# Graph layer with segment maximum: every neighbour row fetched by GpSimd, none rebuilt by TensorE

## What is computed

```
theta_x = (x[dst] - x[src]) @ theta_w.T + theta_b
phi_x   = x[src] @ phi_w.T + phi_b
e       = relu(theta_x + phi_x)
out     = segment_max(e, dst)          # nodes without an edge: 0
result  = layernorm(x + out)
```

## Time and profile before

| | before |
|---|---|
| median of 3 runs | 1052.79 us |
| the profiled execution's own time | 1051.62 us |
| its span, first to last instruction | 1049.1 us |
| mean granted TensorE clock | 0.848 of full speed |
| busy: GpSimd (POOL) | 780.5 us, 74% of the span |
| busy: TensorE (PE) | 705.6 us, 67% |
| busy: VectorE (DVE) | 642.4 us, 61% |
| busy: ScalarE (ACT) | 326.6 us, 31% |
| moved by DMA | 250.69 MB, mean 239 GB/s |

### The profile page before, as it was taken

The page is one execution under the profiler, slowest core; times in us unless marked ns, Lnnn a source line. Parts: engine busy times, 40 slices in busy tenths (PEclk is TensorE's granted clock), DMA queues, the critical chain, the costliest instruction groups (busy, mean ns, idle before and its releaser), DMA issues. The chain is left out here.

```text
span 1049.1 us, 11163 instructions
## 1 busy us (share of the span) xinstructions
PE 705.6 (67%) x3067; PEld 372.2 (35%) x3067; DVE 642.4 (61%) x1563; ACT 326.6 (31%) x708; POOL 780.5 (74%) x812
## 2 busy tenths in 40 slices
PE   5922445999799979875878687768949875663000
PEld 4821223544455544332333233323413333452000
DVE  5006777666666657655655566556556555568698
ACT  2314555433433343213222222222121111110366
POOL 6777777777777777777777777777777777776773
PEclk9965556999889999996999799979979997887555
DMA  8967888767777777777677777777766668985365
GB/s 264 381 228 247 260 265 277 257 226 241 231 237 240 238 239 230 236 245 230 222 231 247 234 234 231 241 233 232 243 224 212 221 213 306 289 295 183 119 198 178
DMA packets 120775, 250.69 MB, mean 239 GB/s; under 512 B 19349, under 2 KB 61290, under 8 KB 120714
## 3 DMA queue, kind: packets, MB, share of 16 engines
q1 hardware_dynamic: 81498, 143.40, 38.6%
q0 software_dynamic: 38640, 105.53, 34.3%
q10 hardware_dynamic: 576, 1.06, 0.4%
HBM read 134.50 MB, written 115.45 MB: 238 GB/s over the span
## 5 line engine op out<-in xcount | busy, mean ns | idle before, releaser
L408 POOL DMA_INDIRECT rows<-b_table,idx x703 | 679.1, 966 | 214.1 <-issue 186.7
L602 PE MATMUL ps_a<-work,shared 128*128 128x512 bf16 x2058 | 480.8, 389 | 72.1 <-DVE work L784 72.0
L480 ACT COPY hist<-acc 128x512 f32<-128x512 f32 x253 | 148.3, 586 | 534.1 <-DVE hist L751 534.1
L602 PEld LDWEIGHTS ps_a<-work,shared 128*128 128x128 bf16 x2058 | 198.6, 100 | 324.5 <-issue 61.8
L751 DVE SCALAR_TENSOR_TENSOR acc<-hist,reset,rows 128x256 f32<-128x256 f32 x173 | 85.5, 494 | 254.1 <-issue 146.9
L751 DVE SCALAR_TENSOR_TENSOR acc<-acc,reset,rows 128x256 f32<-128x256 f32 x253 | 124.7, 493 | 28.6 <-DMA rows<-b_table,idx 16.0
L751 DVE SCALAR_TENSOR_TENSOR hist<-acc,reset,rows 128x256 f32<-128x256 f32 x253 | 122.4, 484 | 26.6 <-DVE acc L751 0.9
L578 PE MATMUL ps_b<-diff_sb,conv_t 128*128 128x256 f32 x204 | 69.5, 473 | 67.0 <-ACT conv_t L472 67.0
L784 DVE TENSOR_SCALAR work<-short_sources,node 128x512 bf16<-128x512 int16 x343 | 113.9, 372 | 0.0
L626 PE MATMUL ps_a<-theta_sb,shared 128*128 128x256 f32 x196 | 54.9, 433 | 38.1 <-DVE shared L822 29.4
L578 PEld LDWEIGHTS ps_b<-diff_sb,conv_t 128*128 128x128 f32 x204 | 45.4, 234 | 81.4 <-ACT conv_t L472 71.9
(11 more groups left out here) (138 smaller groups left out, 498.4 us busy)
## 6 DMA issues: line engine op xcount, KB each, us to landing
runmax<-hist SPq DMA_DIRECT2D x260, 384.0 KB, 3.0
rows<-b_table,idx POOLq DMA_INDIRECT x703, 3.4
b_table<-rows SPq DMA_DIRECT2D x7, 896.0 KB, 9.1
shared<-in_xt SPq DMA_DIRECT2D x49, 128.0 KB, 4.3
work<-b_table SPq DMA_DIRECT2D x24, 256.0 KB, 3.7
early<-in_x SPq DMA_DIRECT2D x12, 512.0 KB
out<-hist SPq DMA_DIRECT2D x11, 512.0 KB, 3.3
shared<-in_xt SPq DMA_DIRECT2D x7, 512.0 KB, 8.7
```

The lines of the kernel that those rows point to most:

```text
L408: pool.indirect_dma_start(out=rows[:, PLACE[k], :], out_offset=None, in_=b_table, in_offset=bass.IndirectOffsetOnAxis(ap=idx[:, k:k + 1], ...
L480: nc.scalar.copy(hist[:, slot:slot + n - 1, :], acc[:, at:at + n - 1, :]).then_inc(s_copied, 1)
L602: mm = pe.matmul(ps_a[k][:].rearrange("p j d -> p (j d)"), split[:, part, t, k * P:(k + 1) * P], hot[:, i % HOT, :], start=(t == 0 and par ...
```

## The change

All 28 steps that TensorE rebuilt are gathered by GpSimd like the others, except that the number of early steps goes from 51 to 53, beginning with group 6. So there are 53 early gathers and 729 gathers from the table. The one-hots, the products, the read-back and splitting of the table, the source loads and the transposes of the products are gone. The conversion of an early row is placed otherwise: TensorE's product for row e - 1 stands directly ahead of the transposes of row e, in group 2 e.

The marks take one pass. VectorE makes `from_tile`, the `dst` indices less 128 t as bf16 (exact where they matter), from an int16 copy of the indices; TensorE multiplies by it once, in the group after the mark (5 + 4 t); ScalarE's signs go to an SBUF tile of bf16 rather than back to PSUM. Part A is spread over groups 204 to 252, one tile per group. Its inputs have a buffer of their own, so that the first 14 tiles are loaded right after the table is written.

```diff
-EARLY = 51
-EARLY_GROUPS = [8 + 2 * e for e in range(EARLY)]
-SPLITS = 3
-AT_ONCE = 4
-HOT = 6
-PRODUCT_SPANS = ((27, 61, 6), (61, 95, 6), (95, 123, 6), (123, 151, 6), (151, 179, 6), (179, 205, 6), (205, 231, 5))
+EARLY = 53
+EARLY_GROUPS = [6 + 2 * e for e in range(EARLY)]
...
+    CONVERT_AT = {2 * e: e for e in range(EARLY)}
     MARK_AT = {4 + 4 * t: t for t in range(NT)}
+    SPREAD_AT = {5 + 4 * t: t for t in range(NT)}
...
-    A_AT = {A_FROM + i: [t for t in (2 * i, 2 * i + 1) if t < NT] for i in range((NT + 1) // 2)}
+    A_AT = {204 + t: t for t in range(NT)}
...
-    GATHERED = [k for k in range(STEPS) if k not in EARLY_OF and k not in PRODUCT_OF]
+    GATHERED = [k for k in range(STEPS) if k not in EARLY_OF]
...
-            for i in range(2):
-                load_pair(i)
+            sp.wait_ge(s_bmm, NT)
+            for t in range(2 * CHUNK):
+                load_tile(t)
             for g in range(NG):
-                if 1 <= g < PAIRS - 1:
-                    load_pair(g + 1)
-                if g in SOURCES_AT:
...
+                if g in A_AT and A_AT[g] + 2 * CHUNK - 2 < NT and A_AT[g] >= 2:
+                    load_tile(A_AT[g] + 2 * CHUNK - 2)
...
-                    nc.scalar.copy(split[:, 1, 2 * i:2 * i + n, :], rest[:, i % 2, 0:n]).then_inc(s_split2, 1)
-                    nc.scalar.copy(split[:, 0, 2 * g:2 * g + n, :], b_pair[:, g % 2, 0:n]).then_inc(s_split1, 1)
+                if g in CONVERT_AT:
+                    e = CONVERT_AT[g]
+                    if e:
+                        act.wait_ge(s_cb, e)
+                        nc.scalar.copy(early[:, e - 1, :], ps_b[:, 0, :]).then_inc(s_cbe, 1)
                     act.wait_ge(s_ct, e + 1)
                     nc.scalar.copy(conv_t[:].rearrange("p k n -> p (k n)"), ps_t[:, 0, :]).then_inc(s_cte, 1)
...
-                    nc.scalar.activation(dst_rows[:, 0:STEPS], dst_rows[:, 0:STEPS], ACT.Sign, bias=node_up[:, t:t + 1],
+                    nc.scalar.activation(signs[:], dst_rows[:, 0:STEPS], ACT.Sign, bias=part_up[:, 0:1],
...
-                        pe.matmul(dst_rows[:, at:at + n], row_of[:], hi[:, at:at + n], start=True, stop=False)
-                        pe.matmul(dst_rows[:, at:at + n], row_of[:], lo[:, at:at + n], start=False, stop=True)
+                        pe.matmul(dst_rows[:, at:at + n], row_of[:], from_tile[:, at:at + n], start=True, stop=True)
...
-                            mm = pe.matmul(ps_a[k][:].rearrange("p j d -> p (j d)"),
-                                           split[:, part, t, k * P:(k + 1) * P], hot[:, i % HOT, :],
-                                           start=(t == 0 and part == 0), stop=(t == NT - 1 and part == SPLITS - 1))
...
-                    nc.vector.scalar_tensor_tensor(split[:, 2, 2 * i:2 * i + n, :], split[:, 1, 2 * i:2 * i + n, :],
-                                                   -1.0, rest[:, i % 2, 0:n], ALU.mult, ALU.add).then_inc(s_split3, 1)
-                    nc.vector.scalar_tensor_tensor(rest[:, i % 2, 0:n], split[:, 0, 2 * i:2 * i + n, :], -1.0,
-                                                   b_pair[:, i % 2, 0:n], ALU.mult, ALU.add).then_inc(s_rest, 1)
-                    nc.vector.tensor_scalar(hot[:, i % HOT, :], short_sources[:, b % 2, :], node[:, t:t + 1], None,
-                                            ALU.is_equal).then_inc(s_hot, 1)
+                    nc.vector.tensor_scalar(from_tile[:], short_dst[:], float(-P * t), None, ALU.add).then_inc(s_from, 1)
```

More of the change, by code:

```diff
@@ L127, in build @@
         late_by_p = runmax[P * KEPT:P * STEPS].rearrange("(p k) d -> p k d", p=P)
[L129 to L143, removed]
+        xt_sb = sb("xt_sb", [P, 2 * CHUNK, KC, P])
         theta_sb = sb("theta_sb", [P, KC, D])
@@ L163, in build @@
         last_node = sb("last_node", [P, NT])
[L164 to L165 removed]
+        part_up = sb("part_up", [P, 1])
         in_row = sb("in_row", [P, NT])
@@ L327, in load_tile @@
                     sp.wait_ge(s_amm, t - 2 * CHUNK + 1)
-                sp.dma_start(late_flat[:, t % (2 * CHUNK)],
+                sp.dma_start(xt_flat[:, t % (2 * CHUNK)],
                              xt[t].rearrange("p k n -> p (k n)")).then_inc(s_at[t % (2 * CHUNK)], 16)
[L331 to L341, removed]
-            for i in range(2):
-                load_pair(i)
-            for g in range(NG):
-                if 1 <= g < PAIRS - 1:
-                    load_pair(g + 1)
-                if g in SOURCES_AT:
[L348 to L357, removed]
+            sp.wait_ge(s_bmm, NT)
+            for t in range(2 * CHUNK):
+                load_tile(t)
+            for g in range(NG):
                 n, slot = STOP[g] - START[g], g % HELD * GROUP
@@ L562, in _, with product @@
             pe.wait_ge(s_xrows, 16 * EARLY)
+            def product(e):
+                pe.wait_ge(s_cte, e + 1)
+                if e:
+                    pe.wait_ge(s_cbe, e)
+                for k in range(KC):
+                    mm = pe.matmul(ps_b[:, 0, :], conv_t[:, k, :], diff_sb[:, k, :],
+                                   start=(k == 0), stop=(k == KC - 1))
+                mm.then_inc(s_cb, 1)
             for g in range(NG):
-                if g in TURN_ROW_AT:
-                    e = TURN_ROW_AT[g]
+                if g in CONVERT_AT:
+                    e = CONVERT_AT[g]
                     if e:
-                        pe.wait_ge(s_cte, e)
+                        product(e - 1)
                     for k in range(KC):
@@ L571, in _ @@
                     mm.then_inc(s_ct, 1)
-                if g in TURNED_ROW_AT:
-                    e = TURNED_ROW_AT[g]
-                    pe.wait_ge(s_cte, e + 1)
-                    if e:
-                        pe.wait_ge(s_cbe, e)
-                    for k in range(KC):
-                        mm = pe.matmul(ps_b[:, 0, :], conv_t[:, k, :], diff_sb[:, k, :],
-                                       start=(k == 0), stop=(k == KC - 1))
-                    mm.then_inc(s_cb, 1)
-                if g in MARK_AT:
-                    t = MARK_AT[g]
+                if g == 2 * EARLY:
+                    product(EARLY - 1)
+                if g in SPREAD_AT:
+                    t = SPREAD_AT[g]
+                    pe.wait_ge(s_from, t + 1)
                     pe.wait_ge(s_rowof, t + 1)
@@ L667, in _ @@
             nc.vector.tensor_copy(p_col[:], part[:])
-            then(nc.vector.tensor_scalar(small[:, 11:12], part[:], 0.5, None, ALU.add))
-            nc.vector.tensor_scalar(node[:], cols[:, 0:NT], float(P), part[:, 0:1], ALU.mult, ALU.add)
-            nc.vector.tensor_scalar(node_up[:], cols[:, 0:NT], float(P), small[:, 11:12], ALU.mult, ALU.add)
+            nc.vector.tensor_scalar(part_up[:], part[:], 0.5, None, ALU.add)
             nc.vector.memset(edges[:, 0:1], 0.0)
@@ L742, in _ @@
                         dve.wait_ge(s_got_end, 16)
-                    elif k in PLACE and (s == 0 or START[g] not in PLACE and s == 1):
+                    elif k in PLACE and (s == 0 or START[g] in EARLY_OF and s == 1):
                         dve.wait_ge(s_got[g % LANDED], ARRIVED[g])
@@ L819, in _ @@
                     nc.vector.memset(x_sb[96:P, NT - 1, :], 0.0).then_inc(s_pad, 1)
-                for t in A_AT.get(g, []):
+                if g in A_AT:
+                    t = A_AT[g]
                     dve.wait_ge(s_amm, t + 1)
```

148 lines of the change are left out of this document (16 added, 132 removed).

## The result

The changed kernel takes 1076.66 us (median of 4 runs, 1075.97 to 1077.83), the kernel before 1053.32 us beside it (4 runs). The ratio is 1.0224, 95% interval 1.0201 to 1.0247: slower, by 23.3 us of the medians. Forecast were 1079 us and a range of 1072 to 1088. The profiled execution took 1075.97 us with a span of 1074.1.

What follows compares the result with a forecast made beforehand. The prediction took GpSimd's full queue of indirect DMAs as the bound: gathers +35.0, splits gone -5.9, one-hots gone -3.9, marks +1.3, the rest 0, made +26.5 us, hence 1079 us, range 1072 to 1088.

Steps and rivals of the forecast that it cites:

- The bound: GpSimd's queue of indirect DMAs runs without waits, so time is their number times their period; net change +26.5 us.
- The price of a gather: On GpSimd's queue, 28 more gathers cost a full 1.25 us period each, nothing hiding them: +35.0 us.
- The fourth rival: GpSimd's gather period falls with TensorE and VectorE lighter; at 1.222 us the time is 1052.8 us; chance 0.03.
- the first: All lengthening of GpSimd's gathers goes, as folds start between gather starts: +20.5 us, 1073.3 us; chance 0.19.
- the second: Lengthening per gather stays, as earlier folds hit gathers where splits did: +35.6 us, 1088.4 us; chance 0.13.
- The third rival: VectorE's new mark instruction hits a gather every time: 19.6 us in place of 1.3, 1097.6 us; chance 0.07.
- The lengthening: Gathers' excess over 1.25 us periods beside VectorE work: from 14.5 to 6.0 us (splits -5.9, one-hots -3.9, marks +1.3).
- The marks: VectorE's new instruction, 49 times at 0.53 us, lying mostly between two gather starts, lengthens gathers: +1.3 us.
- The late groups: Last stretch of table gathers: 0.99 us above the floor before; folds and late passes, 4.7 us in all, stay.
- The folds ahead of them: VectorE folds before the last groups keep lengthening gathers, within 4.7 us for all folds and late passes.
- Conversion, part A, loads: Beside GpSimd's queue: early-row conversion 3.5 us per 6.25 us of gathers, cost 0; part A and loads 0 (-0.5 to +0.5).
- the closing part: From the first gather of node maxima to the end: same code, stays at 77.5 us, change 0.

Runs made afterwards that it cites:

- e3_splits: Changed kernel with only the 50 VectorE split instructions added, on constant data, no table read back; 1261.31 us against 1303.33 for the kernel before on the same slower chip.
- e5_marks_on_scalar: Changed kernel with the new mark instruction made by ScalarE rather than VectorE; 1076.67 us in a single execution, the kernel before 1051.31 beside it.

## Why the prediction was right

**The bound.** The wait view and the starts show GpSimd's queue full from the first gather to the last, before and after. That is the step on which all else rests, and it held: the last table gather starts 26.00 us later, 26.5 forecast.

**The price of a gather.** 28 x 1.25 = 35.0 us. The floor stands in the changed kernel as before: median 946 ns in both, 1.25 us between starts. The fourth rival, a quicker period with TensorE and VectorE lighter, needed 1.222; with TensorE at 29% busy and its clock at half, gathers are not one nanosecond quicker in the median. The other three rivals are out by the same excess of 6.34 us over 728 periods: the first needed 0, the second 15.0 (728 x 0.0206), the third 24.3.

**The lengthening.** 14.5 us before, 6.0 forecast for after, 6.34 measured. By a count over the timeline of the changed kernel, 48 gathers ahead of the last eight groups start inside a fold that reads two operands from SBUF (2.5 us), 37 inside the new mark instruction (1.9 us, 16 of them by more than 0.03), and in the last eight groups 12 inside folds and second passes (2.0 us). The forecast of 6.0 was 4.7 for folds and late passes and 1.3 for marks. Three parts of it were off, and that they came within 0.34 us together is luck:
- The marks cost 1.9 us, not 1.3. The instruction is shorter than estimated, 0.368 us instead of 0.53 for 782 columns, but is hit far more often: the prediction placed it mostly between two starts, and a gather starts inside 37 of the 49. Starts spread evenly would hit 49 x 0.368 / 1.25 = 14. The third rival was near this; what it had wrong is how much of the instruction is left by then: less than 0.13 us in 20 of the 37, which lengthens nothing.
- The late groups cost 2.0 us instead of 1.0 in the whole last stretch: the folds and passes lie in a fixed rhythm against the gathers, and from 967 us on two of three are lengthened. That part A has gone from these groups may be the reason, which no run shows.
- The folds ahead of them cost 2.5 us, and not the 3.7 that they cost before.

Here is the rhythm, in the changed kernel's timeline; five such pairs of lengthened gathers follow one another from 967 to 985 us:

```profile
975.58 0.48 DVE L612 SCALAR_TENSOR_TENSOR hist<-hist,reset,rows 128x256 f32<-128x256 f32 x1
975.72 1.16 POOL L330 DMA_INDIRECT rows<-b_table,idx  x1 [0.30 <-DMA runmax<-hist]
...
977.01 0.48 DVE L621 SCALAR_TENSOR_TENSOR late_max<-hist,is_fix,late_max 128x256 f32<-128x256 f32 x1
977.18 1.14 POOL L330 DMA_INDIRECT rows<-b_table,idx  x1 [0.30 <-DVE hist L612]
```

That VectorE's instruction is the cause and not a companion is shown by `e3_splits` (put back alone, the long gathers return) and by `e5_marks_on_scalar` (taken off VectorE, its 1.9 us go, of which 0.5 come back through `row_of`). The measured size is: a gather that finds the instruction running is longer by what is left of it less 0.13 us (0.125 to 0.14 in the lengthened gathers of the changed kernel).

The rule of the Trainium skill ("SBUF — State Buffer", box on VectorE blocking a DMA) names such a mechanism for VectorE's modes that take both port pairs. The one-hots and marks, with one tensor operand, lengthen gathers as it says; which mode they ran in, no trace tells. For two operands in SBUF the page's own list puts such a lock only against GpSimd instructions that read SBUF. The gathers here, which take their indices from a tile in SBUF, are delayed by them (1.43 us beside L637).

**Conversion, part A, loads: 0.** GpSimd never waited for a fold beyond the 0.3 us, so nothing reached the path. TensorE's clock fell to its lower level, a conversion took 2.07 us and kept up.

**The 2.6 us** by which 1079.3 missed the median are, but for 0.5, in the profiled execution: table gathers began 0.86 us earlier than 71.38 (0.4 of it because the first early gather started at 3.8 us, the rest because fewer early gathers were lengthened), +0.34 by the lengthening, +0.10 before and -1.10 in the closing part, and -0.65 around the span (1.87 us in place of 2.52): -2.2 on the profiled execution. In the closing part the forecast was no change; 77.5 us in `e5_marks_on_scalar` suggests that the 1.1 us are a single execution's. The other 0.5 us are the distance from the profiled execution to the median, 0.69 us after and 1.17 before.

Not shown on a chip like the first: that unused products leave the time alone, and with it that the lower clock has no part in the 23 us, and that 12 gathers more or 8 fewer cost or bring 1.25 us each. The wait view of the changed kernel says the first, the sum of this change is one measurement of the second.

## What to carry to other kernels

Where one engine's queue is full without a wait, as here, the time is the number of its instructions times their period, and some 500 us of work taken off TensorE and VectorE bring back only what that work did to the period: here 8 of 35 us. Check that the queue really is full by the longest wait, not by its busy share (74% before and after). And check it on the machine at hand: the same two programs stand at 1.022 where the queue is full and at 0.978 where other engines hold it up.

## What was not expected of the hardware

- Two chips on which the kernel before takes 24% to 26% longer (1302 and 1327 us against 1053) and the changed one 18% (1270 against 1077). In their traces an update of a semaphore can stand 24 us behind the matmul that gives it, and ScalarE waits for up to 17.6 us at a time (24.6 with products added), while the DMAs' packets take no longer than elsewhere.
- A VectorE instruction int16 to bf16 with a constant added takes 0.368 us for 782 columns, the one that compares with a value per partition 0.346 us for 512.
- A VectorE instruction with two operands in SBUF lengthens an indirect DMA on GpSimd that starts while it runs, by what is left of it less 0.13 us, at 0.35 us (`row_of` in `e5_marks_on_scalar`) as at 0.68 us. The conversions from int16 with one tensor operand do the same; a fold with one operand in PSUM does not (208 such gathers in the changed kernel, none longer than 0.955 us).
